# Patch embedding: split fp32r operands and three products per step against a repacked fp32 tile and one product per step

## The reference, cut to what matters here

```python
patches = X.reshape(B, C, N_PATCHES, PATCH, N_PATCHES, PATCH)
patches = patches.transpose(0, 2, 4, 1, 3, 5).reshape(B, N_PATCHES * N_PATCHES, IN_D)
tokens = jnp.einsum('bpi,hi->bph', patches, W) + b
```

## Time and profile before

| | us |
|---|---|
| median of three runs (3875.5 to 3880.21) | 3876.37 |
| the profiled execution | 3886.44 |
| its span, first to last instruction | 3884.6 |
| patch embedding: start to the first load of the second stage (L382) | 306.12 |
| TensorE busy in the span | 3481.7 |

### The profile page before, as it was taken

How to read it: one execution, slowest core, us unless ns; L and a number is a source line. 1 busy time by engine, 2 the same in 40 slices (tenths; PEclk the granted TensorE clock), 3 DMA queues, 4 the chain that set the end, 5 groups by cost and what they waited for, 6 DMA issues and landing times.

```text
span 3884.6 us, 66340 instructions
## 1 busy us (share of the span) xinstructions
PE 3481.7 (90%) x22496; PEld 2907.9 (75%) x22496; DVE 2225.5 (57%) x4469; ACT 1810.0 (47%) x2931; POOL 1190.5 (31%) x1192
## 2 busy tenths in 40 slices
PE   4776899999999999999999999999999999999998
PEld 3665777777777777777777777777777777787776
DVE  6884455555555555555555555555555555555554
ACT  6882244444444444444444444444444444444445
POOL 0000133332233333332233333223333333223335
PEclk9997899999999999999999999999999999999999
DMA  7761000000000000000000000000000000000000
GB/s 191 152 147 34 8 10 9 5 6 9 9 7 9 9 9 9 5 6 9 9 7 9 9 9 8 6 7 9 7 9 9 9 9 8 6 7 9 7 8 5
DMA packets 165392, 79.34 MB, mean 20 GB/s; under 512 B 81631, under 2 KB 163871, under 8 KB 165023
## 3 DMA queue, kind: packets, MB, share of 16 engines
q1 hardware_dynamic: 162946, 72.99, 9.0%
q10 hardware_dynamic: 2416, 5.97, 0.5%
HBM read 60.65 MB, written 14.97 MB: 19 GB/s over the span
## 4 chain that ended last, share of the span: by engine, by line
issue 56%; POOL 21%; PE 10%; DVE 2%; SPq 1%; ACT 1%; POOLq 1%; DMA 0%; ACTq 0%; DVEq 0%
POOL gelu L908 20%; PE bank L434 3%; PE bank L510 1%; PE bank L475 1%; PE bank L463 1%; POOL gst L921 1%; PE bank L533 1%; PE bank L534 1%; PE bank L469 1%; PE bank L443 1%; SPq L393 1%; POOLq L907 1%; ACT gelu L842 1%; PE bank L447 1%; PE bank L444 1%
## 5 line engine op out<-in xcount | busy, mean ns | idle before, releaser
L908 POOL TENSOR_TENSOR gelu<-gelu 128x386 f32<-128x386 f32 x1024 | 1031.0, 1015 | 2116.6 <-ACT gelu L842 2110.2
L841 ACT ACTIVATE gelu<-bank,b_s 128x386 f32<-128x386 f32 x1024 | 595.6, 582 | 1334.4 <-DVE gelu L626 1328.2
L434 PE MATMUL bank<-gelu,w_s 128*128 128x386 f32 x2048 | 832.5, 493 | 31.8 <-POOL gelu L908 28.5
L626 DVE TENSOR_TENSOR gelu<-bank,ratio 128x386 f32<-128x386 f32 x1024 | 564.1, 555 | 465.7 <-PE bank L447 459.9
L842 ACT ACTIVATE gelu<-gelu,b_s 128x386 f32<-128x386 f32 x1024 | 623.6, 609 | 0.0
L443 PE MATMUL bank<-x_hi,w_hi 128*128 128x386 f32 x1024 | 523.5, 511 | 51.5 <-ACT gelu L841 47.7
L533 PE MATMUL bank<-k_f,q_bd 128*128 128x193 f32 x1600 | 510.5, 401 | 48.4 <-DMA a_bd<-u_scratch 48.4
L533 PEld LDWEIGHTS bank<-k_f,q_bd 128*128 128x128 f32 x1600 | 463.4, 332 | 69.8 <-DMA a_bd<-u_scratch 39.8
L534 PE MATMUL bank<-rw,a_bd 128*128 128x193 f32 x1600 | 514.0, 403 | 0.0
L727 DVE TENSOR_REDUCE mx<-bank 128x2 f32<-128x386 f32 (+1 forms) x416 | 226.0, 543 | 456.0 <-PE bank L534 456.0
L534 PEld LDWEIGHTS bank<-rw,a_bd 128*128 128x128 f32 x1600 | 460.4, 336 | 0.0
(11 more groups left out here) (146 smaller groups left out, 4901.4 us busy)
## 6 DMA issues: line engine op xcount, KB each, us to landing
xt<-in_x SPq DMA_DIRECT2D x192, 196.0 KB
q_bd<-q_f SPq DMA_DIRECT2D x512, 6.2 KB
a_bd<-u_scratch SPq DMA_DIRECT2D x256, 25.0 KB, 2.2
txt_s<-in_txt SPq DMA_DIRECT2D x32, 128.0 KB, 2.2
rv<-in_rel_v ACTq DMA_DIRECT2D x1, 3200.0 KB, 18.7
u_scratch<-k_f SPq DMA_DIRECT2D x32, 100.0 KB, 2.2
u_scratch<-q_f SPq DMA_DIRECT2D x32, 100.0 KB, 2.2
out<-o_s SPq DMA_DIRECT2D x64, 48.5 KB
```

The costliest lines, as they stand in the source:

```text
L434: mm(yb[:, 0:T2], w2_s[:, f, :], gelu1[:, f % RING, :], start=(f == 0), stop=(f == NF - 1)).then_inc(S["w2_done"], 1)
L626: v.tensor_tensor(gelu2[:, f % RING, :], zb[f % 2][:, 0:T2], ratio[:, :], ALU.mult).then_inc(S["z2_done"], 1)
L841: a(gelu1[:, f % RING, :], zb[f % 2][:, 0:T2], ACT.Gelu, bias=b1_s[:, f:f + 1]).then_inc(S["g_done"], 1)
L908: g.tensor_tensor(gelu1[:, f % RING, :], gelu1[:, f % RING, :], gelu2[:, f % RING, :], ALU.add).then_inc(S["hs_done"], 1)
```

## The change

Instead of three fp32r products of split operands, each step is one product in plain fp32: `wt` and `xs` are fp32 tiles of 84 partitions.

- `xs` has two slots. It is the repacked `xt`: ScalarE copies quarters 0 and 1 (`act_packed`), VectorE copies quarters 2 and 3 with `tensor_copy` (`dve_packed`), both at once.
- Both engines start on block i when all of block i-2's products are done (`x_used`) and block i has landed (`x_in`).
- SP loads block i+2 into the slot of `xt` when both have packed block i. The store moves from SP's queue to ScalarE's, behind `copy_tokens`.
- The weights have a tile of their own, with no split; the memsets and the wait for `w_ready` go.

```diff
-        wt_hi, wt_lo = sb("wt_hi", [P, PATCH, P], F32R), sb("wt_lo", [P, PATCH, P], F32R)
-        xt = sb("xt", [ROWS, 2, NB0 * NP_ * IMG])
-        xh, xl = sb("xh", [P, PATCH, n], F32R), sb("xl", [P, PATCH, n], F32R)
+        wt = sb("wt", [ROWS, PATCH, P])
+        xt = sb("xt", [ROWS, 2, n * PATCH])
+        xs = sb("xs", [ROWS, 2, PATCH, n])
...
-            load(sp, 0, 0)
-            sp.wait_ge(w_ready, 1)
-            load(sp, 1, 1)
+            for slot in range(2):
+                load(sp, slot, slot)
             with sp.Fori(0, NT0 // 2 - 1) as k:
                 for slot in range(2):
-                    sp.wait_ge(lo_ready, k * (2 * PARTS0) + (slot + 1) * PARTS0)
+                    sp.wait_ge(act_packed, k * 4 + 2 * slot + 2)
+                    sp.wait_ge(dve_packed, k * 4 + 2 * slot + 2)
                     load(sp, k * 2 + 2 + slot, slot)
-                    store(sp, k * 2 + slot, slot)
...
-                    for q in range(PARTS0):
-                        pe.wait_ge(lo_ready, k * (2 * PARTS0) + slot * PARTS0 + q + 1)
-                        for s in range(q * QS, (q + 1) * QS):
-                            o = ps[slot][:, 0:n]
-                            mm(o, wt_hi[:, s, :], xh[:, s, :], start=(s == 0), stop=False)
-                            mm(o, wt_hi[:, s, :], xl[:, s, :], start=False, stop=False)
-                            m = mm(o, wt_lo[:, s, :], xh[:, s, :], start=False, stop=(s == PATCH - 1))
-                        m.then_inc(part_used, 1)
+                    for s in range(PATCH):
+                        if s % QS0 == 0:
+                            half, part = divmod(s // QS0, 2)
+                            pe.wait_ge((act_packed, dve_packed)[half], k * 4 + 2 * slot + part + 1)
+                        m = nc.tensor.matmul(ps[slot][:, 0:n], wt[:, s, :], xs[:, slot, s, :], start=(s == 0), stop=(s == PATCH - 1))
+                    m.then_inc(x_used, 1)
...
+            def pack(k, slot):
+                act.wait_ge(x_used, k * 2 + slot + 1)
+                act.wait_ge(x_in[slot], k * X_ALL + X_ALL)
+                for s in (0, QS0):
+                    nc.scalar.activation(xs[:, slot, s:s + QS0, :], steps(slot, s, s + QS0), ACT.Copy).then_inc(act_packed, 1)
...
+            pack(0, 0)
             with act.Fori(0, NT0 // 2 - 1) as k:
-                split(k + 1, 0, lambda: copy_tokens(k, 1))
-                split(k + 1, 1, lambda: copy_tokens(k + 1, 0))
+                pack(k, 1)
+                copy_tokens(k, 0)
+                pack(k + 1, 0)
+                copy_tokens(k, 1)
...
-                    for q in range(PARTS0):
-                        dve.wait_ge(hi_ready, k * (2 * PARTS0) + slot * PARTS0 + q + 1)
-                        w = slice(q * QS, (q + 1) * QS)
-                        v.tensor_tensor(xl[0:ROWS, w, :], part_of(slot, q), xh[0:ROWS, w, :].bitcast(F32), ALU.subtract).then_inc(lo_ready, 1)
+                    dve.wait_ge(x_used, k * 2 + slot + 1)
+                    dve.wait_ge(x_in[slot], k * X_ALL + X_ALL)
+                    for s in (HALF, HALF + QS0):
+                        nc.vector.tensor_copy(xs[:, slot, s:s + QS0, :], steps(slot, s, s + QS0)).then_inc(dve_packed, 1)
```

More of the change, by code:

```diff
@@ L67 @@
 NT0 = B // NB0
-PARTS0 = 4
+QS0 = PATCH // 4
 CO = {}
@@ L132, in patch_embed @@
         n = NB0 * NPATCH
-        wt_hi, wt_lo = sb("wt_hi", [P, PATCH, P], F32R), sb("wt_lo", [P, PATCH, P], F32R)
-        xt = sb("xt", [ROWS, 2, NB0 * NP_ * IMG])
-        xh, xl = sb("xh", [P, PATCH, n], F32R), sb("xl", [P, PATCH, n], F32R)
+        wt = sb("wt", [ROWS, PATCH, P])
+        xt = sb("xt", [ROWS, 2, n * PATCH])
+        xs = sb("xs", [ROWS, 2, PATCH, n])
         tok = sb("tok", [P, 2, n])
-        wt = xt[:, 1, 0:PATCH * P].rearrange("p (s h) -> p s h", h=P)
         ps = [ctx.enter_context(nc.psum_tensor(f"tok_ps{i}", [P, 512], F32)) for i in range(2)]
-        zeroed, w_in, w_hi_ready, w_ready = sem("zeroed"), sem("w_in"), sem("w_hi_ready"), sem("w_ready")
-        tok_copied, hi_ready, lo_ready, part_used = (
-            sem(n_) for n_ in "tok_copied hi_ready lo_ready part_used".split())
+        w_in, x_used, tok_copied, act_packed, dve_packed = (
+            sem(n_) for n_ in "w_in x_used tok_copied act_packed dve_packed".split())
         x_in = [sem(f"x_in{i}") for i in range(2)]
@@ L145, in patch_embed @@
         block = ctx.enter_context(nc.Block())
-        QS = PATCH // PARTS0
+        HALF = PATCH // 2
+        X_ALL = 16 * C_IN * NB0
         def load(sp, i, slot):
@@ L153, in load, with steps @@
                     sp.dma_start(dst.rearrange("r (y w) -> r y w", w=IMG), src).then_inc(x_in[slot], 16)
[L155 to L162, removed]
+        def steps(slot, s0, s1):
+            return xt[:, slot, :].rearrange("p (n s) -> p s n", s=PATCH)[:, s0:s1, :]
         @block.sync
         def _(sp):
-            sp.dma_start(wt, a["w_tok"]).then_inc(w_in, 16)
-            load(sp, 0, 0)
-            sp.wait_ge(w_ready, 1)
-            load(sp, 1, 1)
+            sp.dma_start(wt[:, :, :], a["w_tok"]).then_inc(w_in, 16)
+            for slot in range(2):
+                load(sp, slot, slot)
             with sp.Fori(0, NT0 // 2 - 1) as k:
                 for slot in range(2):
-                    sp.wait_ge(lo_ready, k * (2 * PARTS0) + (slot + 1) * PARTS0)
+                    sp.wait_ge(act_packed, k * 4 + 2 * slot + 2)
+                    sp.wait_ge(dve_packed, k * 4 + 2 * slot + 2)
                     load(sp, k * 2 + 2 + slot, slot)
-                    store(sp, k * 2 + slot, slot)
[L176 to L185, removed]
         @block.tensor
         def _(pe):
-            mm = nc.tensor.matmul
-            pe.wait_ge(w_ready, 1)
+            pe.wait_ge(w_in, 16)
             with pe.Fori(0, NT0 // 2) as k:
@@ L216, in _ @@
                 act.dma_start(R["rw"][r:P - 7 + r:8, :], a["rel_rev"][:, c0:c0 + RW]).then_inc(R["const_in"], 16)
-            act.wait_ge(w_in, 16)
-            act.wait_ge(zeroed, 4)
-            nc.scalar.activation(wt_hi[0:ROWS, :, :], wt, ACT.Copy).then_inc(w_hi_ready, 1)
+            def pack(k, slot):
[3 more added lines that the diff above has]
+                    nc.scalar.activation(xs[:, slot, s:s + QS0, :], steps(slot, s, s + QS0), ACT.Copy).then_inc(act_packed, 1)
@@ L222, in copy_tokens @@
             def copy_tokens(k, slot):
-                act.wait_ge(part_used, k * (2 * PARTS0) + (slot + 2) * PARTS0)
+                act.wait_ge(x_used, k * 2 + slot + 3)
                 act.wait_ge(tok_out[slot], k * 16 + 16)
                 nc.scalar.activation(tok[:, slot, :], ps[slot][:, 0:n], ACT.Copy).then_inc(tok_copied, 1)
-            def split(k, slot, before_last):
-                act.wait_ge(x_in[slot], (k + 1) * (16 * C_IN * NB0))
-                for q in range(PARTS0):
[L233 to L236, removed]
@@ L238, in _ @@
-            split(0, 0, lambda: None)
-            split(0, 1, lambda: copy_tokens(0, 0))
-            with act.Fori(0, NT0 // 2 - 1) as k:
-                split(k + 1, 0, lambda: copy_tokens(k, 1))
-                split(k + 1, 1, lambda: copy_tokens(k + 1, 0))
+                act.wait_ge(tok_copied, k * 2 + slot + 3)
+                act.dma_start(tok_scratch[:, bass.ds(k * (2 * NB0) + slot * NB0, NB0), :],
+                              tok[:, slot, :].rearrange("p (b n) -> p b n", b=NB0)).then_inc(tok_out[slot], 16)
@@ L243, in _ @@
+            pack(0, 0)
+            with act.Fori(0, NT0 // 2 - 1) as k:
+                pack(k, 1)
+                copy_tokens(k, 0)
+                pack(k + 1, 0)
+                copy_tokens(k, 1)
+            pack(NT0 // 2 - 1, 1)
+            copy_tokens(NT0 // 2 - 1, 0)
             copy_tokens(NT0 // 2 - 1, 1)
+            for slot in range(2):
+                act.wait_ge(tok_out[slot], NT0 // 2 * 16 + 16)
         @block.vector
         def _(dve):
-            v = nc.vector
-            for x in (xh, xl):
-                v.memset(x[64:P, :, :].bitcast(F32), 0.0).then_inc(zeroed, 1)
@@ L250, in _ @@
-            dve.wait_ge(w_hi_ready, 1)
-            v.tensor_tensor(wt_lo[0:ROWS, :, :], wt, wt_hi[0:ROWS, :, :].bitcast(F32), ALU.subtract).then_inc(w_ready, 1)
             dve.sem_inc(tok_copied, 2)
-            dve.sem_inc(part_used, PARTS0)
+            dve.sem_inc(x_used, 2)
             for slot in range(2):
```

## The result

The changed kernel takes 3998.55 us (median of four runs, 3998.25 to 4001.08) against 3878.29 us on the same chip: ratio 1.0312, 95% interval 1.0294 to 1.033. It is 120 us slower, where the forecast was 57 faster.

A forecast was written before the change was run, and what follows sets the result against it. Bound before: ScalarE and VectorE chained with the load; after: transfers at 12.9 us a block. Block 15 lands at 230.0, TensorE ends at 246.6, second stage starts at 249.2, not 306.1: 56.9 us less, 3820 us, range 3809 to 3845.

The forecast's parts named there:

- TensorE's: Patch embedding's plain fp32 products: 28 x 0.436 = 12.2 us a block, at most 13.4, against 10.1 before.
- the transfers: Patch embedding's new bound: 12.9 us a block for loads and token stores, with TensorE at 12.2 close behind.
- Rival C: Patch embedding: a wait per block leaves TensorE at half clock, 24.4 us a block, 129 us slower, 4005; chance 4%.
- The prediction's sign for 3813: In the patch embedding, no TensorE wait and DMA share below 0.95 mean TensorE sets the pace, time near 3813.
- the wait of 0.9 us: TensorE's wait at 121 us in the kernel before; clock stayed 1.00, read as disagreeing with the skill's half-clock rule.
- Elementwise: Patch embedding's packing copies: 3.68 us each on ScalarE, 3.64 on VectorE, two per block, running beside TensorE's previous block.
- The loads: Patch embedding: 2.54 MB a block in 12.9 us, between 12.1 and 13.7, loads continuous with 3 us of slack.
- the case the forecast put near 3813: Patch embedding at 12.1 us a load: TensorE decides, second stage starts at 243.1, 63 us less.
- The start: Block 0: images land at 36.86, table load 1.28, first quarter packed at 41.7, half clock costs 2.1 us, end 56.0.
- rival A: Patch embedding: loads don't overlap (28 us less, 3848) or clock halves each block (33 less, 3843); chance 10%.
- rival B: Patch embedding: shared memory use keeps a block at 16 to 17 us, nothing moves; chance 3%.

The follow-up runs named there:

- 96-row kernel: Changed kernel with `wt` and `xs` on 96 partitions instead of 84, twelve rows of zeros: 3813.65 us, ratio 0.9846 to the kernel before.
- the traced run with no wait at the handover: Changed kernel with 350 fp32r products of 128 rows ahead, running into the 84-row products without a wait: 3813.3 us over five runs, ratio 0.9835.

## Why the prediction was wrong

**The term that failed is TensorE's: 28 x 0.436 = 12.2 us a block, a price at 2.4 GHz.** The step behind it was that 84 instead of 128 partitions change nothing; the runs show that 84-row products never got the higher clock. At 1.2 GHz it is 28 x 0.851 = 23.8 us; 16 blocks of it are 381, and with 42.7 for the start and 2.6 for the end the stage is 426, against 427.98 measured. The stage was forecast at 249.2, 179 too short. This term alone is worth 187.5 us, from 240.46 with 96 rows to 427.98; the transfers, which the forecast had setting the pace, were priced some 9 us too dear, the other way.

**Where the reading went astray.** The forecast priced 84 rows by L578, whose 65 rows cost no more than L577's 128, and concluded that fewer rows change nothing. That is right for the length of a product at a given clock (the 84-row products after 128-row ones took the same 0.215 us) and says nothing on what clock the products get: in the rows L578 runs between L577's 128-row products, in a stream that already had it. The kernel before had a sign to be priced, the memsets of 44 partitions that no data needs; the forecast counted them only as work that goes.

**The clock** was weighed only by TensorE's waits. Rival C put 4005 us on a clock that stays low, within 7 us of the 3998.55 measured, but its mechanism was a wait in each block, and TensorE had none after 42.7 us. The price was right, the cause wrong, and that they meet is luck; its 4% weighed that mechanism alone. The prediction's sign for 3813, no wait of TensorE and a DMA share below 0.95, failed for the same reason: there was no wait, the share was 0.47, and the time was 3998.55.

The Trainium skill (TensorE: Matmul & The Clock Gate, "HAM oscillation") speaks of matmuls that lose the clock by waiting for a DMA; the changed kernel never waited once it had begun and never had the clock, so the section doesn't cover this case. In the loop that this section of the Trainium skill shows, the DMA waits are some 3 to 5 us long, so the wait of 0.9 us is not the disagreement that the prediction took it for.

**What held, as the 96-row kernel shows**, which is the changed kernel with the one cause taken away:

- Elementwise: 3.54 us a copy on ScalarE (3.68 taken), 3.48 on VectorE (3.64 taken). Both off the path, as forecast.
- TensorE at 2.4 GHz: 0.431 us a step in the window (0.436 taken).
- The loads: 218 GB/s at a share of 0.98, so 2.54 MB take 11.7 us. The forecast's 12.9, midway between 13.7 from 186 GB/s and 12.1 from the busy share, was too dear; the lower end was nearer. So TensorE, not the transfers, sets the pace, the case the forecast put near 3813.
- The start: images at 37.43 (36.86 taken), then the table load, 1.28 us, in the path as forecast. The low clock at the start lasted from 42.25 to 46.1 us, which costs 1.9 us (2.1 taken).
- The second stage starts at 240.46 us; the forecast had 249.2, and 243.1 with TensorE setting the pace.
- The time: 3813.65 us, 61 us below the 3874.47 of before on that chip, for a forecast of 57 in its likeliest case and 63 in its cheapest.

In the 96-row kernel rival A (loads that don't overlap) and rival B did not come about: the DMA share is 0.98 and TensorE works without a break.

## What to carry to other kernels

Before a product loses rows (padding left out, a shorter contraction), ask whether the stream around it has anything else that gets the clock up; a price taken from a short product among full ones doesn't answer that. Here 12 rows of zeros (84 to 96) moved the start of the second stage from 427.98 to 240.46 us. Read the clock from the distance between products, here 0.4255 or 0.215 us a record, and don't trust a granted clock of 1.00 before the first stretch below it.

## What the runs showed of the hardware

- With 64, 84 and 88 rows in use TensorE's clock stayed at 1.2 GHz through a stage in which it worked without a break for 383 us; with 96, 112 and 128 it rose to 2.4 GHz at 46.1, 47.7 and 46.6 us and stayed there. Rows of zeros count as rows in use.
- It is the same for fp32r: with 84 rows each of the 448 products of one line took 415 or 416 ns, with 128 rows their median was 283.
- A clock once raised held through 190 us of 84-row products in the traced run with no wait at the handover; all five runs took the time that goes with it.
- VectorE's fp32 copy of 84 x 1792 elements, read 28 elements apart, took 3.43 us, against 3.64 us for the two-input subtraction of the same shape: one input less brought 6%.
